# Setup of a fused cross-attention and mixture-of-experts kernel: order of the normalising, the maxima and the second batch's queries

## The chip, the cores and the metric

One core of one Trainium2 chip. The time is device microseconds of one execution, as the median of the runs shown; lower is better. TensorE is called PE in the profile, VectorE DVE, ScalarE ACT, GpSimd POOL, SyncE SP.

## The reference

```python
# x (2, 512, 128); ctx (2, 154, 128); H = 16 heads of 8; E = 8 experts, 2 chosen, capacity 160
x = x + tanh(g_xattn) * attention(layernorm(x), ctx, ctx, Wq, Wk, Wv, Wo)   # causal mask
x = x + tanh(g_ffn) * moe(layernorm(x), Wr, W1, b1, W2, b2)

# attention: softmax(where(causal, Q K^T / sqrt(8), -inf)) V, heads joined, @ Wo.T
# moe: softmax router, two experts of each token, their weights normalised, rank within an
#      expert by cumulated sum, tokens over the capacity dropped, gelu between W1 and W2
```

All in float32. The attention's queries are 512 rows for each of two batches (four tiles of 128 rows), its keys 154 (128 and 26 more). The reference's softmax subtracts the row's maximum of the scores.

## The kernel before, in words

One program with hand-written queues for each engine, ordered by semaphores. It has a setup (until 20 us), eight attention groups (20 to 72 us), and the mixture of experts (72 to 140 us). The change touches the setup and the lists of banks in the groups.

**Setup.** SP loads X for the first batch (L366), the context (L368, L369), X for the second batch (L370), WV; then, when POOL has made zeros (`zero_ready`), it clears the tables `slots` and `results` in DRAM (L374, L379). ACT issues the loads of WK and WQ (L595, L596), clears `v_all` and `top` (L599) and copies the keys (L606). DVE clears the selection matrices (L1513, L1514), does the statistics of both batches (`statistics`, L1305: four bn_stats, four bn_aggr, an add of epsilon), normalises the first (`layernorm`, L1316), splits the keys into a high and a low part (L1524, L1525), makes the masked keys of heads 0 to 5 for the maxima (L1526), normalises the second batch (L1530). The reciprocal root is a POOL power (`root`, L451). POOL makes identities and masks (L425 to L462), then after both roots the selection matrices (`packing`, L443), copies of the last context rows (L471), masked keys of heads 6 to 15 (`keys_for_max`, L474), the ones beside the values (L484 to L490), `block_mask`, the key mask `mask_k1` (L498 to L502) and `ones` (L503), which increments `consts3`; then `k1` of both batches (L507) and the masked keys of the second batch.

The PE runs matmuls on zeros (L820), the keys (L825), filling matmuls (`fill`, L805, calls L844 and L846), transposes the normalised rows (`turn_rows`, L834), makes the queries (`queries`, L826), and then alternates four packings of keys (`pack_keys`, L852; ACT copies each at L622) with seven banks of maxima (L1039 to L1053); the second batch's rows and queries and the projected values (`project_values`, L1026) lie between them. ACT copies the high half of queries (L614), DVE subtracts it for the low half (`low_queries`, L1532).

**Banks of maxima.** Two PSUM banks, `turn`, are passed between the PE and their readers in the order of the list `turns`. A bank of maxima holds the scores of one tile of 128 queries against up to four heads' masked keys (`maxima`, L865: one matmul L873, a mask on tile 0, L876, and on tile 1, L879); DVE reduces it to one maximum for each head into `top` (L1328) and frees it. Tile 0 has 128 keys and four heads (512 columns), the others 154 keys and three heads (462) or two (308). There are 22 banks for a batch, 44 in all; `shares` says how many are done in the setup (7) and beside each group (8, 6, 6, 6, 5, 5, 1), and `maxima_beside` at which of six places of the group.

**A group** is four heads of one batch. In the PE's order (L1059 to L1100): maxima at place 0, `scores` (L899), maxima at 1, `last_scores` of the last 26 keys (L910), maxima at 2, `pack` of the next group (L1018: two matmuls of the queries L886, then four of the maxima L892, for which it waits until `top` is written), maxima at 3, `values` of the group before (L920), maxima at 4, `last_values` (L933), maxima at 5. `scores` waits for ACT's copy of the pack (L644). ACT does two exponentials of a group (L681), one of the last keys (L684), then the copy of the next pack. DVE does the reductions in the same order, and between them the folds and the router.

Before group 0 the PE waits for `consts3` (L1058); the second batch's queries (L1054) and the wait for their two halves (L1070) come before `last_scores` of group 0.

Of the kernel before, what the change touches and what calls it, by code (L numbers as in the profile page):

```python
# [35 lines left out]
P = 128  # L36
B, S, D = 2, 512, 128
C = 154
# [30 lines left out]
def groups_of_heads(qt):  # L69

    if qt == 0:
        return [(4 * n, 4, P) for n in range(4)]
    return [(0, 3, C), (3, 3, C), (6, 3, C), (9, 3, C), (12, 2, C), (14, 2, C)]


def build(nc, x, ctxT, gx, gf, wqT, wkT, wvT, woT, wr, w1, b1T, w2, b2T, out):
    with ExitStack() as stack:
# [37 lines left out]
        mask_k1 = sb("mask_k1", [P, 32], BF16)  # L115
# [16 lines left out]
        kT = sb("kT", [P, B, CP])  # L132
# [110 lines left out]
        def w2_part(e):  # L243
# [12 lines left out]
        x_in = [sem(f"x_in{b}") for b in range(B)]  # L256
# [4 lines left out]
        zero_ready = sem("zero_ready")  # L261
# [55 lines left out]

        maxima_todo = [(b, qt, *h) for b in range(B) for i in range(4) for qt in range(QT)
                       for h in groups_of_heads(qt) if h[0] // 4 == i]

        shares = (7, 8, 6, 6, 6, 5, 5, 1)
        maxima_first = maxima_todo[:shares[0]]
        FIRST_HEADS = 6
# [41 lines left out]
        def _(sp):  # L365
            sp.dma_start(X[:, 0:QT, :], x_d[:, 0:QT, :]).then_inc(x_in[0], 16)  # L366
# [3 lines left out]
            sp.dma_start(X[:, QT:NT, :], x_d[:, QT:NT, :]).then_inc(x_in[1], 16)  # L370
            sp.dma_start(WV[:, :], wvT).then_inc(wv_in, 16)

            sp.wait_ge(zero_ready, 1)
# [6 lines left out]

            for g in range(TOPK):
                clear_table(g)
# [33 lines left out]
        def _(pool):  # L416
            steps = [0]

            def step(ins):
# [5 lines left out]
            pool.memset(zeros[:, :], 0.0)  # L425
            step(pool.memset(slot0[:, :], 0.0))
            step(pool.memset(slot0[:, D:D + 1], FAR))
            pool.memset(half[:, :], -0.5).then_inc(zero_ready, 1)  # L428
# [8 lines left out]
                               channel_multiplier=-1).then_inc(consts1, 1)  # L437
            step(pool.memset(minus_raw[:, :, :], 0.0))
            step(pool.affine_select(out=minus_raw[:, :, :], in_=minus_raw[:, :, :], compare_op=ALU.not_equal,
                                    fill=-1.0, base=-3 * HD, pattern=[[-32, 4], [-1, 2]],  # L440
                                    channel_multiplier=1))
# [9 lines left out]
            def root(tiles, n):  # L451
# [5 lines left out]

            step(pool.memset(mask_q[:, :, :], 0.0))
            pool.affine_select(out=mask_q[:, :, :], in_=mask_q[:, :, :], compare_op=ALU.is_ge, fill=NEG,
                               base=0, pattern=[[0, 4], [-1, P]], channel_multiplier=1)  # L460
            pool.tensor_copy(identr[:, :], identf[:, :])
            pool.tensor_copy(identb[:, :], identf[:, :]).then_inc(consts2, 1)  # L462
# [11 lines left out]
            def keys_for_max(b, h0):  # L474

                pool.tensor_tensor(kTr[:, b, h0:H],  # L476
                                   kT_part[:, 0, b, 0:C].unsqueeze(1).to_broadcast([P, H - h0, C]),
                                   head_mask[:, :, :].rearrange("p i j -> p (i j)")[:, h0:H].unsqueeze(2)
                                   .to_broadcast([P, H - h0, C]), ALU.mult).then_inc(kTr_ready, 1)

            pool.wait_ge(kT_split, 1)
            keys_for_max(0, FIRST_HEADS)

            pool.wait_ge(zeroed, 1)  # L484
            for r in range(2):
                c = ONES_AT[r]
                step(pool.memset(v0[:, :, :, :].rearrange("p b (n r) d -> p b n r d", r=2)[:, :, :, r, c:c + 1], 1.0))
                for j in range(4):
                    step(pool.memset(v1[32 * j:32 * j + C1, :, :, j, :].rearrange(
                        "p b (n r) d -> p b n r d", r=2)[:, :, :, r, c:c + 1], 1.0))  # L490
# [103 lines left out]
        def _(act):  # L594
# [41 lines left out]

            turned_rows(1)
            place_values()
            high_queries(1)

            def pack(g):

# [1119 lines left out]
```

## Time and profile before

| what | us |
|---|---|
| median of 3 runs | 143.41 |
| the runs | 142.35 to 143.93 |
| the profiled execution, its own time | 142.3 |
| its span in the profile | 140.2 |
| granted TensorE clock, mean | 0.993 of 2.4 GHz |

The span runs from the first to the last record of the profile; 2.1 us of the execution lie around it. Times of rows are microseconds from the span's start.

### The profile page before, as it was taken

Reading aid. Unit: us, or ns where it says so; the run is one execution under the profiler, and the core shown is the slowest. Engines: PE = TensorE matmul, PEld = TensorE weight load, DVE = VectorE, ACT = ScalarE, POOL = GpSimd, SP = SyncE. Lnnn points to the kernel's source line nnn. Section 1 sums busy time; section 2 is a strip of 40 time slices with the busy share of each in tenths; the row PEclk is TensorE's granted clock in tenths of the full one; section 3 lists DMA queues with packets and bytes.
Section 4 is the critical chain, followed back from the end, with each engine's and each line's share of the span. In section 5 each row is a group of like instructions: output and inputs, shape, how many; then the busy total and the mean of one; then the engine's idle time right before and its main releaser. Section 6 shows DMA issues by size and latency. Waiting matters only on the chain.

```text
span 140.2 us, 2241 instructions
## 1 busy us (share of the span) xinstructions
PE 124.4 (89%) x715; PEld 86.4 (62%) x715; DVE 103.2 (74%) x259; ACT 73.7 (53%) x134; POOL 84.0 (60%) x126
## 2 busy tenths in 40 slices
PE   5998988899899999999989989969779999989930
PEld 2443844455455646675369448959579999977620
DVE  5599845948584647377969788974399998999381
ACT  4924667166361447154827778632587678721110
POOL 6679779999999141004285788871067878773000
PEclk9999999999999999999999999999999999999997
DMA  3899880003240000000089411111740101010805
GB/s 97 257 212 222 210 269 23 0 0 99 69 134 0 5 0 0 0 0 2 0 226 314 162 58 39 39 57 55 158 114 10 45 31 43 28 35 26 293 8 150
DMA packets 19018, 12.22 MB, mean 87 GB/s; under 512 B 3381, under 2 KB 16999, under 8 KB 19008
## 3 DMA queue, kind: packets, MB, share of 16 engines
q1 hardware_dynamic: 17344, 9.59, 26.7%
q0 software_dynamic: 1088, 1.86, 4.0%
q10 hardware_dynamic: 576, 0.66, 1.3%
q8 instruction: 5, 0.08, 0.2%
q14 instruction: 5, 0.04, 0.1%
HBM read 7.25 MB, written 5.06 MB: 88 GB/s over the span
## 4 chain that ended last, share of the span: by engine, by line
PE 43%; POOL 17%; DVE 11%; DMA 11%; issue 11%; ACT 2%; SPq 2%; POOLq 1%; DVEq 0%
POOL slots L555 6%; PE turn L873 6%; PE sc L1205 5%; PE av L929 5%; DVE top L1328 4%; PE av L937 4%; PE turn L886 3%; DMA xn_all<-results 3%; PE sc L1221 3%; DMA X<-x 2%; POOL results L587 2%; PE sc L905 2%; PE turn L892 2%; POOL shared L476 2%; DMA parts_all<-slots 2%
## 5 line engine op out<-in xcount | busy, mean ns | idle before, releaser
L1328 DVE TENSOR_REDUCE top<-turn 128x3 fp32r<-128x462 f32 (+2 forms) x44 | 26.2, 606 | 13.8 <-PE turn L873 7.2
L587 POOL DMA_INDIRECT results<-p,result_of x18 | 19.8, 1099 | 12.6 <-DVE p L1630 8.1
L681 ACT ACTIVATE p_all<-sc 128x1024 f32<-128x1024 f32 x16 | 15.5, 1022 | 16.2 <-PE sc L905 16.1
L873 PE MATMUL turn<-shared,q_all 128*128 128x462 f32 (+2 forms) x44 | 20.4, 468 | 2.3 <-DVE top L1328 0.8
L555 POOL DMA_INDIRECT slots<-rows,slot_of x16 | 18.4, 1148 | 5.3 <-issue 5.0
L1205 PE MATMUL sc<-q_all,w_all 128*128 128x320 f32 x96 | 17.4, 320 | 1.2 <-issue 0.8
L752 ACT ACTIVATE late<-sc,B 128x320 f32<-128x320 f32 x32 | 15.0, 523 | 3.5 <-PE sc L1205 3.5
L1205 PEld LDWEIGHTS sc<-q_all,w_all 128*128 128x128 f32 x96 | 14.2, 188 | 2.3 <-issue 2.0
L873 PEld LDWEIGHTS turn<-shared,q_all 128*128 128x128 f32 x44 | 8.3, 189 | 11.4 <-ACT q_pack_all L644 4.7
L546 POOL TENSOR_SCALAR_AFFINE_SELECT p_all<-p_all 128x512 f32<-128x512 f32 x8 | 5.2, 646 | 16.7 <-ACT p_all L681 16.7
L1647 DVE TENSOR_TENSOR shared<-late,shared 128x640 fp32r<-128x640 f32 x16 | 13.1, 821 | 0.3
L929 PE MATMUL av<-p_all,late 128*32 128x512 f32 x64 | 8.5, 604 | 0.2 <-POOL p_all L546 0.2
L808 PE MATMUL sc<-mask_q,identb 128*128 128x512 bf16 x32 | 7.7, 380 | 0.0
L476 POOL TENSOR_TENSOR shared<-kT_part,head_mask 128x1540 fp32r<-128x1540 f32 (+1 forms) x2 | 7.1, 3534 | 0.0
L454 POOL TENSOR_TENSOR rstd<-mean_var,half 128x4 f32<-128x4 f32 x4 | 4.2, 1040 | 4.9 <-DVE mean_var L1314 3.7
L937 PE MATMUL av<-p,late 128*128 128x384 f32 x16 | 6.8, 505 | 0.0
L644 ACT ACTIVATE q_pack_all<-turn 128x512 fp32r<-128x512 f32 x8 | 4.8, 600 | 3.8 <-PE turn L892 3.8
L886 PE MATMUL turn<-q_all,pack_q 128*128 128x512 f32 x16 | 6.1, 464 | 0.4
L665 ACT ACTIVATE late<-av 128x512 f32<-128x512 f32 (+1 forms) x5 | 2.5, 511 | 6.8 <-PE av L937 6.8
L820 PE MATMUL sc<-zeros 128*128 128x512 f32 (+1 forms) x6 | 4.2, 868 | 1.5 <-POOL half L428 1.5
L538 POOL TENSOR_TENSOR w_all<-W,w_all 128x512 fp32r<-128x512 f32 x4 | 5.1, 1281 | 0.3
L892 PEld LDWEIGHTS turn<-identr,top 128*128 128x128 f32 x32 | 4.7, 190 | 1.0 <-DVE top L1328 0.3
(255 smaller groups left out, 283.1 us busy)
## 6 DMA issues: line engine op xcount, KB each, us to landing
W<-w SPq DMA_DIRECT2D x8, 256.0 KB, 3.1
p_all<-w SPq DMA_DIRECT2D x8, 256.0 KB, 5.2
slots<-slot SPq DMA_DIRECT2D x1, 1386.0 KB, 11.0
results<-zeros SPq DMA_DIRECT2D x2, 512.0 KB, 9.7
parts_all<-slots SPq DMA_DIRECT2D x5, 198.0 KB, 2.9
X<-x SPq DMA_DIRECT2D x2, 256.0 KB, 3.6
xn_all<-results SPq DMA_DIRECT2D x2, 256.0 KB, 3.9
xn_all<-results ACTq DMA_DIRECT2D x2, 256.0 KB, 4.2
```

The source lines that it names most:

```text
L476: pool.tensor_tensor(kTr[:, b, h0:H], kT_part[:, 0, b, 0:C].unsqueeze(1).to_broadcast([P, H - h0, C]), head_mask[:, :, :].rearrange("p i j ...
L555: nc.gpsimd.indirect_dma_start(out=slots, out_offset=bass.IndirectOffsetOnAxis(ap=slot_of[:, c:c + 1], axis=0), in_=rows[:, t, :], in_offs ...
L587: nc.gpsimd.indirect_dma_start(out=results, out_offset=bass.IndirectOffsetOnAxis(ap=result_of[0:m, e, n:n + 1], axis=0), in_=y[0:m, e % 2, ...
L681: act.activation(p0[:, t, heads, :], sc[:, heads, :], ACT.Exp, scale=SCALE).then_inc(sc_free, 1)
L752: act.activation(hT[:, e % 2, c, :], sc[:, c, 0:SLOTS], ACT.Gelu, bias=B1[:, e, c:c + 1]).then_inc(h_ready, 1)
L873: mm = pe.matmul(o, qT[:, 0, b, qt * P:qt * P + P], kTr[:, b, h0:h0 + nh, 0:keys], start=True, stop=(qt >= 2), skip_group_check=True)
L886: pe.matmul(ps, pack_q[:, part, i].rearrange("p j s d -> p (j s d)"), qT[:, part, b, :], start=(part == 0), stop=False, skip_group_check=True)
L929: pe.matmul(av[32 * j:32 * j + VW, :], v0[:, b].rearrange("p h d -> p (h d)")[:, at:at + VW], p0[:, g % 2, j, :], start=(g % 2 == 0), stop ...
L937: pe.matmul(av[:, P:S], v1[:, b].rearrange("p i j d -> p (i j d)")[:, at:at + 4 * VW], p1[:, g % 2, :], start=False, stop=True, skip_group ...
L1205: mm = pe.matmul(sc[:, c, 0:SLOTS], w1_part[:, e, wp, c * P:c * P + P], xsT[:, e % 2, xp, :], start=(wp == xp == 0), stop=(wp == 1))
L1328: dve.tensor_reduce(top[:, qt, h0:h0 + nh, 3 * HD], ps[:, 0:nh * keys].rearrange("p (h k) -> p h k", h=nh), AX.X, ALU.max).then_inc(turn_f ...
L1647: dve.tensor_tensor(hT_part[:, t, 1, c:c + 2, 0:SLOTS], h, hT_part[:, t, 0, c:c + 2, 0:SLOTS], ALU.subtract).then_inc(h_split, 1)
```

## The change

- X of the first batch is loaded in two pieces, tiles 0 and 1 by SP and tiles 2 and 3 by ACT's queue ahead of WK and WQ. The semaphore of the second batch is the third.
- POOL no longer makes `slot0` and the ones beside the values; DVE does (ten small memsets before the first normalising). The clearing of `slots` waits for DVE's `slot_zeros`, that of `results` for `zero_ready`.
- POOL's order: identities, head mask, `minus_raw`, the key selection matrix, `identb`, root of the first batch, `mask_q`, `identr`, the query selection matrix, the masked keys of heads 4 to 9, root of the second batch, block mask, `ident4`, a key mask of 32 partitions with one affine select, `ones`, `k1` of batch 0, masked keys of heads 10 to 15, `k1` of batch 1, masked keys of batch 1.
- DVE's order: statistics and normalising of the first batch (a signal for each tile), then the keys, masked keys of heads 0 to 3, statistics of the second batch, low queries of the first, five maxima, normalising of the second. The copy `kT` goes: ACT writes the high part of the keys itself, and DVE subtracts it from PSUM.
- PE: 3 and 3 filling matmuls for 12 and 4, with `identb` as moving operand; transposes wait for each tile; order of packings of keys and banks as below; the second batch's transposes behind the first pack (into `av`), its queries behind `last_scores` of group 0. ACT's high half of them comes after the two exponentials of group 0, DVE's low half before the reductions at place 2.
- 20 banks of maxima for a batch, 40 in all: the heads go in threes, and head 3 has one bank for tiles 1 to 3 (three matmuls of 154 columns). Five are done in the setup, and 7, 6, 6, 6, 5, 4, 1 beside the groups. With that, head 7 of tiles 1 to 3 and heads 10 and 11 of tile 3 of the first batch are reduced behind the packs that read them, which take the cleared value there.
- The mask of the last keys is placed by `ident4`, and the tanh of the gates moves behind group 0's exponentials.

```diff
-def groups_of_heads(qt):
-    if qt == 0:
-        return [(4 * n, 4, P) for n in range(4)]
-    return [(0, 3, C), (3, 3, C), (6, 3, C), (9, 3, C), (12, 2, C), (14, 2, C)]
+def units_of_maxima(b, i):
+    first = [(b, (0,), 4 * i, 4, P)]
+    if i == 0:
+        return first + [(b, (qt,), 0, 3, C) for qt in range(1, QT)] + [(b, tuple(range(1, QT)), 3, 1, C)]
+    starts = ((), (4, 7), (10,), (13,))[i]
+    return first + [(b, (qt,), h0, 3, C) for h0 in starts for qt in range(1, QT)]
...
-        shares = (7, 8, 6, 6, 6, 5, 5, 1)
+        shares = (5, 7, 6, 6, 6, 5, 4, 1)
-        FIRST_HEADS = 6
+        FIRST_HEADS = 4
+        NEXT_HEADS = 10
...
 # gpsimd
-            root((0, QT), 1)
-            root((QT, NT), 2)
-            pool.wait_ge(cleared, 1)
-            packing(pack_k, [kp for kp, qp in PRODUCTS]).then_inc(pack_ready, 1)
+            pool.wait_ge(cleared, 1)
+            packing(pack_k, [kp for kp, qp in PRODUCTS]).then_inc(pack_ready, 1)
+            pool.tensor_copy(identb[:, :], identf[:, :]).then_inc(consts2, 1)
+            root((0, QT), 1)
+            step(pool.memset(mask_q[:, :, :], 0.0))
...
-            pool.wait_ge(kT_split, 1)
-            keys_for_max(0, FIRST_HEADS)
+            pool.wait_ge(kT_ready, 1)
+            keys_for_max(0, FIRST_HEADS, NEXT_HEADS)
+            root((QT, NT), 2)
...
 # scalar
+            act.dma_start(X[:, 2:QT, :], x_d[:, 2:QT, :]).then_inc(x_in[1], 16)
             act.dma_start(WK[:, :], wkT).then_inc(wk_in, 16)
...
-            turned_rows(1)
             place_values()
-            high_queries(1)
...
             pack(0)
+            turned_rows(1)
...
                     act.activation(p0[:, t, heads, :], sc[:, heads, :], ACT.Exp,
                                    scale=SCALE).then_inc(sc_free, 1)
+                if g == 0:
+                    high_queries(1)
...
 # tensor
-            fill(sc[:, 3, :], 12)
+            fill(sc[:, 3, :], 3)
             turn_rows(0)
-            fill(sc[:, 3, :], 4)
+            fill(sc[:, 3, :], 3)
+            pe.wait_ge(wq_in, 16)
             queries(0)
...
             pack_keys(0)
-            pe.wait_ge(consts2, 1)
+            pack_keys(1)
+            pe.wait_ge(consts2, 2)
             pe.wait_ge(kTr_first, 1)
             pe.wait_ge(q_high, 1)
-            maxima(maxima_first[0:2])
-            pack_keys(1)
+            maxima(maxima_first[0:1])
+            pack_keys(2)
+            maxima(maxima_first[1:2])
+            pack_keys(3)
             maxima(maxima_first[2:3])
-            pack_keys(2)
-            maxima(maxima_first[3:4])
-            pack_keys(3)
-            maxima(maxima_first[4:5])
-            turn_rows(1)
-            maxima(maxima_first[5:6])
             project_values()
-            maxima(maxima_first[6:])
-            queries(1)
+            maxima(maxima_first[3:])
             pe.wait_ge(pack_ready, 2)
             pe.wait_ge(q_ready, 1)
             pack(0)
-            pe.wait_ge(consts3, 1)
+            pe.wait_ge(v_ready, 5)
+            turn_rows(1)
...
                 if g == 0:
                     pe.wait_ge(k_ready, 1)
-                    pe.wait_ge(q_ready, 2)
+                    pe.wait_ge(consts3, 1)
                 if g < NG:
                     last_scores(g)
+                if g == 0:
+                    queries(1)
...
 # vector
-            dve.wait_ge(x_in[0], 16)
-            statistics((0, QT), X)
-            dve.wait_ge(x_in[1], 16)
-            statistics((QT, NT), X)
-            layernorm((0, QT), X, xn, xn_ready)
+            statistics((0, QT), X, True)
...
+            ones_beside_values()
+            dve.wait_ge(rstd_ready, 1)
...
+            for t in range(QT):
+                normalised_rows(t)
...
+            statistics((QT, NT), X, True)
...
             low_queries(0)
             dve.wait_ge(zeroed, 2)
             maxima(maxima_first)
             pass_bank()
-            low_queries(1)
+            dve.wait_ge(rstd_ready, 2)
+            for t in range(QT, NT):
+                normalised_rows(t)
...
                 maxima(maxima_beside(g, 0))
                 maxima(maxima_beside(g, 1))
+                if g == 0:
+                    low_queries(1)
```

## Rows read from the trace of the kernel before

**Rows 1.** Page, busy time by engine and the group of the reductions.

```profile
PE 124.4 (89%) x715; PEld 86.4 (62%) x715; DVE 103.2 (74%) x259; ACT 73.7 (53%) x134; POOL 84.0 (60%) x126
...
L1328 DVE TENSOR_REDUCE top<-turn 128x3 fp32r<-128x462 f32 (+2 forms) x44 | 26.2, 606 | 13.8 <-PE turn L873 7.2
```

**Rows 2.** Busy time of each engine by stretch, with granted clock and DMA.

```profile
0.00:4.00 4.00, 2.48 (x3) 1.17 (x4) 1.82 (x2) 2.16 (x2) 2.56 (x17) 1.00 0.43 126
...
27.07:33.00 5.93, 5.93 (x38) 3.31 (x37) 3.58 (x9) 3.05 (x5) 5.52 (x15) 1.00 0.00 0
```

**Rows 3.** Timeline of the setup, first batch: start, length, instruction, idle before it.

```profile
4.25 0.87 DVE L1308 BATCH_NORM_STATS2 stats<-X 128x6 f32<-128x128 f32 x4 [1.19 <-DMA X<-x]
...
5.83 1.04 POOL L454 TENSOR_TENSOR rstd<-mean_var,half 128x4 f32<-128x4 f32 x1 [0.80 <-DVE mean_var L1314]
...
7.81 1.11 DVE L1321 TENSOR_SCALAR xn_all<-X,mean_var,rstd 128x128 f32<-128x128 f32 x4
...
9.68 0.60 ACT L610 ACTIVATE xn_all<-sc 128x512 f32<-128x512 f32 x1 [2.52 <-PE sc L838]
...
10.34 1.11 PE L831 MATMUL sc<-xn_all,WKQ 128*128 128x512 f32 x2
...
10.87 1.50 DVE L1321 TENSOR_SCALAR xn_all<-X,mean_var,rstd 128x128 f32<-128x128 f32 x4
...
11.49 0.60 ACT L614 ACTIVATE q_all<-sc 128x512 fp32r<-128x512 f32 x1 [1.22 <-PE sc L831]
```

**Rows 4.** Timeline from the last packing of keys to the first scores.

```profile
15.24 0.53 ACT L622 ACTIVATE w_all<-av,minus_one 128x320 fp32r<-128x320 f32 x1
...
16.03 0.60 PE L1032 MATMUL av<-WV,CT 128*128 128x128 f32 x4
...
18.46 0.56 PE L892 MATMUL turn<-identr,top 128*128 128x128 f32 x4
18.97 0.69 DVE L1534 TENSOR_TENSOR q_all<-sc,q_all 128x512 fp32r<-128x512 f32 x1 [1.00 <-ACT q_all L614]
19.11 0.60 ACT L644 ACTIVATE q_pack_all<-turn 128x512 fp32r<-128x512 f32 x1 [0.17 <-PE turn L892]
...
19.66 0.50 PE L873 MATMUL turn<-shared,q_all 128*128 128x512 f32 x1 [0.64 <-POOL ones L503]
...
20.32 0.51 PE L905 MATMUL sc<-q_pack_all,w_all 32*128 32x512 f32 x4
```

**Rows 5.** Timeline of group 0 to the second scores.

```profile
20.86 1.94 ACT L681 ACTIVATE p_all<-sc 128x1024 f32<-128x1024 f32 x2 [1.06 <-PE sc L905]
...
23.23 0.66 PE L892 MATMUL turn<-identr,top 128*128 128x128 f32 x4
...
27.07 0.50 PE L905 MATMUL sc<-q_pack_all,w_all 32*128 32x512 f32 x4
```

**Rows 6.** Chain that ended last, pieces of groups 1 to 4.

```profile
30.85 0.34 PE turn L873
...
36.54 0.41 PE turn L873
...
42.18 0.39 PE turn L892 x4
...
50.89 0.43 PE turn L873
51.32 0.23 PE turn L876
```

**Rows 7.** Groups of VectorE by form, 12 to 66 us: busy, mean ns, idle.

```profile
L1328 DVE TENSOR_REDUCE top<-turn 128x3 fp32r<-128x462 f32 x24 | 15.1, 641 | 6.1 <-PE turn L873 3.9 <-PE turn L879 2.1
L1328 DVE TENSOR_REDUCE top<-turn 128x2 fp32r<-128x308 f32 x12 | 5.7, 479 | 4.0 <-PE turn L873 3.3 <-PE turn L879 0.2
L1328 DVE TENSOR_REDUCE top<-turn 128x4 fp32r<-128x512 f32 x8 | 5.5, 692 | 3.7 <-PE turn L876 3.7
```

**Rows 8.** Groups by line, 0 to 20.3 us: busy, mean ns.

```profile
L820 PE MATMUL sc<-zeros 128*128 128x512 f32 (+1 forms) x6 | 4.2, 868 | 1.5 <-POOL half L428 1.5
...
L489 POOL MEMSET late<- 26x4 f32 x8 | 0.8, 98 | 0.5
```

More of the change, by code:

```diff
@@ L254, in build @@
         turn = [psum(f"turn{n}", [P, 512]) for n in range(2)]
-        x_in = [sem(f"x_in{b}") for b in range(B)]
+        x_in = [sem(f"x_in{n}") for n in range(3)]
         ctx_in, ctx_rep, wk_in, wv_in, wq_in, wo_in, small_in = (
@@ L423, in step @@
                 pool.wait_ge(pool_step, steps[0])
[L425 to L428, printed above, removed]
+            pool.memset(zeros[:, :], 0.0).then_inc(zero_ready, 1)
+            pool.memset(half[:, :], -0.5)
             pool.memset(identf[:, :], 0.0)
@@ L807, in fill @@
                 for _ in range(n):
-                    pe.matmul(ps, identb[:, :], mask_q[:, :, :].rearrange("p h k -> p (h k)"), start=True, stop=True,
+                    pe.matmul(ps.rearrange("p (n d) -> p n d", n=4), identb[:, :],
+                              identb[:, :].unsqueeze(1).to_broadcast([P, 4, P]), start=True, stop=True,
                               skip_group_check=True)
@@ L865, in maxima @@
             def maxima(todo):
-                for b, qt, h0, nh, keys in todo:
+                for b, tiles, h0, nh, keys in todo:
                     ps = bank()
@@ L871, in maxima @@
                         use_of["maxima", 4 * b + h0 // 4 + 1] = full[0]
[L872 to L880 removed]
+                    for n, qt in enumerate(tiles):
+                        o = ps[:, n * nh * keys:(n + 1) * nh * keys].rearrange("p (h k) -> p h k", h=nh)
+                        mm = pe.matmul(o, qT[:, 0, b, qt * P:qt * P + P], kTr[:, b, h0:h0 + nh, 0:keys],
+                                       start=(n == 0), stop=(qt >= 2), skip_group_check=True)
+                        if qt == 0:
+                            mm = pe.matmul(o, identb[:, :], mask_q[:, 0:nh, :], start=False, stop=True,
+                                           skip_group_check=True)
+                        if qt == 1:
+                            mm = pe.matmul(o[:, :, P:C], identb[:, :], mask_q[:, 0:nh, 0:C1], start=False,
+                                           stop=True, skip_group_check=True)
                     mm.then_inc(turn_full, 1)
@@ L1285, in _ @@
         def _(dve):
-            steps, uses, banks, norms = [0], [0], [0], [0]
+            steps, uses, banks, norms = [0], [0], [0], [2]
             def step(ins):
@@ L1303, in pass_bank, with statistics @@
                 banks[0] += 1
-            def statistics(tiles, src):
+            def statistics(tiles, src, landing=False):
                 for t in range(*tiles):
+                    if landing and t in (0, 2, QT):
+                        dve.wait_ge(x_in[t // 2], 16)
                     last = dve.bn_stats(stats[:, t, :], src[:, t, :])
@@ L1325, in maxima @@
             def maxima(todo):
-                for b, qt, h0, nh, keys in todo:
+                for b, tiles, h0, nh, keys in todo:
                     ps = bank()
-                    dve.tensor_reduce(top[:, qt, h0:h0 + nh, 3 * HD],
-                                      ps[:, 0:nh * keys].rearrange("p (h k) -> p h k", h=nh),
+                    n = nh * len(tiles)
+                    to = top[:, tiles[0], h0:h0 + nh, 3 * HD] if nh > 1 else top[:, tiles[0]:tiles[-1] + 1, h0, 3 * HD]
+                    dve.tensor_reduce(to, ps[:, 0:n * keys].rearrange("p (h k) -> p h k", h=n),
                                       AX.X, ALU.max).then_inc(turn_free, 1)
```

133 lines of the change are left out of this document (66 added, 67 removed).

## The prediction, made before the change was run

> **What bounds the kernel now.** I read the page first: TensorE is busy for 89% of the span, VectorE, ScalarE and GpSimd much less [rows 1]. Then the busy time by stretch: from the first scores to the last it is full. In 27.07 to 33.00 us it is busy in every microsecond, at a granted clock of 1.00, so a microsecond of matmul moved into that stretch costs nearly a microsecond [rows 2]. Third, the timeline of the first 27 us, where no engine is full and the time is a chain of handovers: X lands, statistics, root, normalise, transpose, queries, maxima, first packing, first scores [rows 3, 4]. Before the first scores, at 20.32 us, the PE also waited for POOL's constants: its first bank of group 0 started at 19.66 with `ones` named as what released it [rows 4]. Last the chain of waits: inside the groups a bank of maxima stands on it with 0.34 us where it has two heads and 0.41 to 0.43 where it has three or four [rows 6]. After group 7 nothing is edited. Everything there follows the last group, so I let it shift by whatever group 7 shifts by, and compare the landmarks "first scores" (20.32), "second scores" (27.07) and the groups 1 to 6 after them.
>
> **Setup up to the first queries.** The first root starts at 5.83 and takes 1.04, ending at 6.87, but the normalising starts only at 7.81, since VectorE did the second batch's statistics in between [rows 3]. That order is turned round. X's first tiles come in two pieces on two queues with the same bytes in all; I give that 0.1 us (between 0 and 0.3). Ten small memsets now stand on VectorE between the variance (5.6) and the root's end (6.75). No row has a small memset on VectorE; POOL's take 98 ns each [rows 8], the statistics' single steps (0.87 for four) 0.22 [rows 3]: 1.0 to 2.2 us for ten. I take 1.0, since the count of written elements is as small as POOL's; the root's 1.04 then covers it, and at the other end it would come through with 1.1 us. So normalising starts at 6.8, not 7.81: 1.0 earlier. The old one released a block of four tiles, and the copy of the turned rows started 0.76 after the last tile (8.92 to 9.68) [rows 3]; with a transpose behind each tile only the last is left, about 0.25. The copy starts at 8.2: 1.5 earlier. ScalarE issues one more DMA (the two clears and the copy of kT come 0.5 later, done by 7.7): hidden behind the normalising. Copy 0.60, queries 1.1, copy 0.60 [rows 3]: the high queries are done at 10.6 instead of 12.09.
>
> The second normalising of before ran 1.50 us for the work that took 1.11 in the first [rows 3], with POOL busy beside both; POOL's affine selects of mask_q now run beside the first. The Trainium skill (GPSIMD Engine Reference, Specifications) says why that may be: the SBUF interfaces are shared with VectorE, with contention when VectorE runs in a two-port mode or with two SBUF inputs. By the row of 1.11 the copy is at 8.2; by the rule with the row of 1.50 it is at 8.6, and the setup's gain 0.4 smaller.
>
> **From there to the first scores.** Four packings of keys end, by the last ScalarE copy (15.24 + 0.53), 3.7 after the high queries [rows 3, 4]. Now two packings stand ahead of the first bank and only one bank between the rest: copies of 0.53 one behind another with two round trips of the PE give 2.55, so 13.15. VectorE, with the second statistics (1.5 us) now ahead of the low queries, starts its maxima at 11.75; it isn't what holds this. Projected values: from 16.03 to about 17.05 [rows 4], now to 14.15. Two banks follow: 0.5 for the matmul, two reductions of 0.64 [rows 7] and a handover of 0.1, and the pack of the maxima starts at 16.05 instead of 18.46, ScalarE's copy of it at 16.65 instead of 19.11 [rows 4]. POOL has made its constants by about 14.5 (no ones beside the values, one affine select for the key mask instead of four in a chain) and k1 of the first batch by 15.6, so the wait on `ones` is gone. What is late next is the second batch: VectorE normalises it only after the fifth reduction (15.9), 1.1 us, to 17.0; its transposes stand ahead of group 0 on the PE, and from that group's first bank to the scores it is 0.66 as before (19.66 to 20.32) [rows 4]. First scores at 17.85: **2.45 us earlier**. I hold this good to 0.7 either way.
>
> **Group 0 gives most of it back.** The second batch's queries are now in the group. The PE has room for its 1.0 us. But the order of two other engines binds them: ScalarE does the high half only behind the group's two exponentials, and VectorE does the low half before the reductions of the third and fourth bank, for which the first packing of group 1 waits. From the rows: exponentials start 0.54 after the scores and last 1.94, the high queries 0.60, the low 0.69, two reductions 1.28 [rows 4, 5, 7], the pack of maxima 0.66 [rows 5], and some 0.15 of handovers: 5.85 after the first scores, at 23.7. Before it was 23.23 + 0.66 = 23.89 [rows 5], 3.6 after them. So 2.25 of the 2.45 are gone. Then one bank fewer stands before the second scores, in a stretch paced by reductions of 0.64: second scores at 26.3 instead of 27.07. **0.8 us earlier** is left.
>
> **Groups 1 to 6.** The columns of maxima are the same in all; only their place moves, together with two banks fewer in the setup, one fewer in groups 0 and 5 each. In batch 0 all reductions of two heads (479 ns) become of three (641 ns) [rows 7]; on the PE a bank of three costs 0.07 more than one of two (0.34 against 0.41), and one of four with its mask 0.43 + 0.23 = 0.66, 0.32 more than one of two [rows 6]. Going through the lists: group 1 had one bank of four and five of two, now has two of four and four of three, 0.32 + 4 x 0.07 - small masks = +0.5. Group 2 about +0.2, as its start is where VectorE is behind and two of its reductions are longer. Group 3 has the bank that holds one head for three tiles: three short matmuls instead of one. No row has this form; the nearest above is the pack's four matmuls of 128 columns in 0.39, 0.10 each [rows 6], below it is nothing beyond the columns. Three cost 0.3 against 0.2 and a small mask: +0.2 (0 to 0.3). Group 4 loses a bank of four: -0.25. Group 5: one of two fewer (-0.34), three longer (+0.2), one with a mask (+0.32), in all +0.15. Group 6: +0.05. Sum +0.85.
>
> The packs of groups 1 and 2 don't wait for all the maxima of their heads any more (head 7 of tiles 1 to 3, heads 10 and 11 of tile 3 come behind them; they are taken as cleared), so the change in order adds no wait there but the one on the bank just issued in group 1, hidden by the pack's first 0.73 us. Of POOL's later work all is earlier.
>
> **Sum.** -2.45 + 2.25 - 0.65 (the bank in group 0) + 0.85 = 0 us. The profiled execution took 142.3 us (span 140.2, 2.1 around it) and comes out at 142.3; the median of the runs was 143.41, 1.1 above it. I forecast 143.4 us, no change.
>
> **Rivals.** (A) The bank round trips are the price in the groups too. A reduction takes 0.61 us in the mean and has 0.31 of idle time before it (13.8 us over 44) [rows 1]. If that sets the groups' time and not the columns, the two banks fewer there give 0.92 each, 1.85 in place of the 0.65 of one of them, and the 0.85 of dearer columns isn't paid: with the 0.2 left of the setup that is 2.05 less, so 141.4. For it: setup and group 0 are paced so. Against it: in groups 1 to 6 the PE is full, and the banks that go take no columns with them [rows 2, 6].
> (B) Slower: the PE falls to its lower level in the setup. Twelve of the sixteen filling matmuls ahead of the first transposes and queries go, and from 6.8 us to 16 the PE has gaps. The first matmuls of before, on zeros, took 868 ns each in the mean for 512 columns or fewer [rows 8], against 1.11 for two of 512 at 10.34 [rows 3]: half the rate, though the granted clock reads 1.00 (2.4 GHz) for the first 4 us [rows 2]. At 1.2 GHz from the queries to the first pack, its matmuls on the path (queries 1.1, packings of keys, values 1.0, the pack 1.3) would take some 2 us more: 145.4. It decides if the clock is down at the first queries. The Trainium skill (TensorE: Matmul & The Clock Gate, What's actually happening) says that "the default state is throttled, and activity releases the throttle"; by that rule fewer fills can cost this, and the trace agrees in so far as the first matmuls were slow.
> (C) Slower, less: group 0's loss is as above but the normalising is late by the dear memsets (1.1) and the longer banks stall VectorE in groups 1 and 2 for another 0.5: 145.0.
> (D) The change does what it says: the second queries lie in group 0 for nothing, with the setup's whole 2.45 kept. With the bank and the dearer columns that is -2.45 - 0.65 + 0.85 = -2.25: 141.1. Against it stands only, but firmly, the order on ScalarE and VectorE.
>
> **Chances.** Forecast 0.50, A 0.17, D 0.11, B 0.09, C 0.13. A measurement of this kernel can tell about 1% (1.4 us) from no change. Faster by over 1% takes A and D: 0.28; slower takes B and C: 0.22; within: 0.50. The forecast's own range is 142.3 to 144.5; to take in 8 of 10 it goes from 141.1 to 145.2.
>
> **What would show it.** In the changed profile: normalising at 6.8 with VectorE's memsets done before; the high queries copied at 10.0; the first pack's copy at 16.65; first scores at 17.9; VectorE's low queries of the second batch started some 3.1 us after them, TensorE idle before the pack of group 1; second scores at 26.3; seventh group's scores (66.0 now) within 0.5 of that. Wrong it would be if the second scores came before 25.5 (the reductions didn't wait, or the first scores are earlier), if groups 1 to 6 took less than before (A), if the queries' two matmuls took 1.7 us or more (B), or if normalising started after 7.3 (C).

## The result and the profile after

The changed kernel takes **157.55 us** in the median (157.24 to 158.09, 4 runs), the kernel before 142.91 beside it (142.35 to 143.93). The ratio is 1.106, 95% interval 1.099 to 1.112: 10 to 11% slower. I had forecast 143.4, with 145.2 as the upper end. The runs of one kernel differ by up to 6 us with the mean granted clock of the run, so the column "undisturbed" of the table below takes the runs within 1.5% of the fastest of their kernel, and the ratios are formed over these.

The page of the changed kernel (busy time; granted clock in 40 slices; two groups by line):

```profile
span 156.1 us, 2215 instructions
...
PE 134.4 (86%) x702; PEld 91.4 (59%) x705; DVE 108.8 (70%) x266; ACT 73.7 (47%) x134; POOL 82.6 (53%) x114
...
PEclk9999965555579999999689999999999999999997
...
L1331 DVE TENSOR_REDUCE top<-turn 128x3 fp32r<-128x462 f32 (+1 forms) x40 | 25.6, 649 | 20.5 <-PE turn L874 8.3
...
L1537 DVE TENSOR_SCALAR xn_all<-X,mean_var,rstd 128x128 f32<-128x128 f32 x8 | 8.4, 1128 | 0.0
```

Two things stand out. The clock line has a hole from slice 6 to slice 12, 20 to 45 us. And the normalising, eight small instructions, takes 1128 ns each in the mean, where it took 1.11 us for the first four and 1.50 for the second [rows 3]. The chain of waits has one piece of 6.47 us in it, the longest of the chain:

```profile
14.81 1.19 DVE top L1331 x2
16.00 6.47 DVE xn_all L1537 x3
22.47 0.04 issue
22.51 0.73 PE av L837 x2
```

The timeline of the changed kernel up to the second scores (start, length, instruction, idle time of its engine before it; these answer to rows 3, 4 and 5):

```profile
6.47 1.60 DVE L1537 TENSOR_SCALAR xn_all<-X,mean_var,rstd 128x128 f32<-128x128 f32 x4
...
9.23 1.10 PE L830 MATMUL sc<-xn_all,WKQ 128*128 128x512 f32 x2
...
10.36 0.60 ACT L612 ACTIVATE q_all<-sc 128x512 fp32r<-128x512 f32 x1 [1.28 <-PE sc L830]
...
15.24 1.74 POOL L476 TENSOR_TENSOR shared<-kT_part,head_mask 128x924 fp32r<-128x924 f32 x1
...
15.91 6.80 DVE L1537 TENSOR_SCALAR xn_all<-X,mean_var,rstd 128x128 f32<-128x128 f32 x4
16.82 0.60 ACT L640 ACTIVATE q_pack_all<-turn 128x512 fp32r<-128x512 f32 x1 [1.02 <-PE turn L893]
16.93 1.04 POOL L501 TENSOR_TENSOR shared<-w_all,block_mask 128x512 fp32r<-128x512 f32 x1
...
17.20 0.30 PE L837 MATMUL av<-identf,xn_all 128*128 128x128 f32 x1 [0.48 <-DVE xn_all L1537]
...
18.07 4.31 POOL L476 TENSOR_TENSOR shared<-kT_part,head_mask 128x2464 fp32r<-128x2464 f32 x1
...
18.25 0.33 PE L837 MATMUL av<-identf,xn_all 128*128 128x128 f32 x1 [0.75 <-DVE xn_all L1537]
...
22.51 0.73 PE L837 MATMUL av<-identf,xn_all 128*128 128x128 f32 x2 [3.93 <-DVE xn_all L1537]
...
24.05 0.80 PE L906 MATMUL sc<-q_pack_all,w_all 32*128 32x512 f32 x4 [0.38 <-issue]
...
28.91 0.69 DVE L1556 TENSOR_TENSOR q_all<-av,q_all 128x512 fp32r<-128x512 f32 x1 [2.60 <-ACT q_all L612]
...
30.20 1.22 PE L887 MATMUL turn<-q_all,pack_q 128*128 128x512 f32 x2 [1.19 <-DVE top L1331]
...
35.58 0.80 PE L906 MATMUL sc<-q_pack_all,w_all 32*128 32x512 f32 x4
```

The setup of the first batch is near what I had worked out: the high queries' copy at 10.36 (10.0), the first pack's at 16.82 (16.65). Then read the POOL rows beside VectorE's four. The second and the third of the four, each asked for by itself, and the reduction ahead of them:

```profile
15.37 0.63 DVE L1331 TENSOR_REDUCE top<-turn 128x3 fp32r<-128x462 f32 x1
...
16.98 1.22 DVE L1537 TENSOR_SCALAR xn_all<-X,mean_var,rstd 128x128 f32<-128x128 f32 x1
...
17.97 4.48 DVE L1537 TENSOR_SCALAR xn_all<-X,mean_var,rstd 128x128 f32<-128x128 f32 x1
```

POOL's multiplications end at 16.98 (1.74 from 15.24), at 17.97 and at 22.38; the transposes of the first three tiles start at 17.20, 18.25 and 22.51. So each of the first three normalising instructions ended 0.1 to 0.2 us behind the POOL instruction in flight, and the third fell behind the longest, the masked keys of batch 1. The fourth, behind that one, took 0.33 us. The PE had 0.33 us of work between 18.0 and 20.0 and none in the next two. Busy time by stretch:

```profile
16.00:20.00 4.00, 1.34 (x8) 0.80 (x6) 4.00 (x3) 0.60 (x1) 4.00 (x4) 1.00 0.81 241
20.00:24.00 4.00, 1.16 (x3) 0.72 (x4) 2.71 (x2) 0.60 (x1) 3.94 (x9) 0.60 0.17 49
24.00:44.00 20.00, 18.21 (x50) 9.37 (x52) 7.79 (x13) 6.52 (x10) 9.00 (x14) 0.50 0.10 28
```

After the gap the granted clock is 0.50, 1.2 GHz, for over 20 us, though the PE is busy in 18.21 of 20: group 0 takes 11.5 us (6.75 before) and group 1 9.9 (5.1).

### The profile page after: what moved, and what is told of

Its sections match the earlier page's. It is cut to its first block, busy times and chain, and to the rows that moved or that the text cites. A ratio compares the mean times of both kernels' runs of the same rounds, so it can differ in the third digit from the quotient of the medians.

```text
span 156.1 us, 2215 instructions
## 1 busy us (share of the span) xinstructions
PE 134.4 (86%) x702; PEld 91.4 (59%) x705; DVE 108.8 (70%) x266; ACT 73.7 (47%) x134; POOL 82.6 (53%) x114
## 4 chain that ended last, share of the span: by engine, by line
PE 57%; DVE 12%; issue 8%; POOL 8%; DMA 8%; ACT 2%; SPq 1%; POOLq 1%; DVEq 0%
PE turn L874 8%; POOL slots L551 6%; PE av L930 6%; PE sc L1204 5%; PE av L938 4%; DVE xn_all L1537 4%; PE turn L887 3%; PE sc L821 3%; DMA xn_all<-results 3%; DVE top L1331 3%; PE turn L893 2%; PE sc L906 2%; PE sc L1220 2%; POOL results L583 2%; DMA parts_all<-slots 2%
## 5 line engine op out<-in xcount | busy, mean ns | idle before, releaser
L1331 DVE TENSOR_REDUCE top<-turn 128x3 fp32r<-128x462 f32 (+1 forms) x40 | 25.6, 649 | 20.5 <-PE turn L874 8.3
L874 PE MATMUL turn<-shared,q_all 128*128 128x462 f32 (+2 forms) x44 | 23.2, 554 | 1.0 <-DVE top L1331 0.6
L1204 PE MATMUL sc<-q_all,w_all 128*128 128x320 f32 x96 | 17.4, 320 | 1.5 <-issue 1.0
L874 PEld LDWEIGHTS turn<-shared,q_all 128*128 128x128 f32 x44 | 9.6, 224 | 10.9 <-issue 5.7
L930 PE MATMUL av<-p_all,late 128*32 128x512 f32 x64 | 9.4, 661 | 0.0
L887 PE MATMUL turn<-q_all,pack_q 128*128 128x512 f32 x16 | 6.7, 504 | 2.1 <-DVE top L1331 1.6
L1537 DVE TENSOR_SCALAR xn_all<-X,mean_var,rstd 128x128 f32<-128x128 f32 x8 | 8.4, 1128 | 0.0
L476 POOL TENSOR_TENSOR shared<-kT_part,head_mask 128x924 fp32r<-128x924 f32 (+1 forms) x3 | 7.8, 2590 | 0.0
L893 PEld LDWEIGHTS turn<-identr,top 128*128 128x128 f32 x32 | 5.5, 224 | 1.4 <-DVE top L1331 0.8
L837 PE MATMUL av<-identf,xn_all 128*128 128x128 f32 x4 | 1.4, 390 | 5.2 <-DVE xn_all L1537 5.2
L808 PE MATMUL sc<-identb 128*128 128x512 bf16 x22 | 5.8, 388 | 0.0
```

Of the source, the lines that this page charges most:

```text
L874: mm = pe.matmul(o, qT[:, 0, b, qt * P:qt * P + P], kTr[:, b, h0:h0 + nh, 0:keys], start=(n == 0), stop=(qt >= 2), skip_group_check=True)
L887: pe.matmul(ps, pack_q[:, part, i].rearrange("p j s d -> p (j s d)"), qT[:, part, b, :], start=(part == 0), stop=False, skip_group_check=True)
L930: pe.matmul(av[32 * j:32 * j + VW, :], v0[:, b].rearrange("p h d -> p (h d)")[:, at:at + VW], p0[:, g % 2, j, :], start=(g % 2 == 0), stop ...
L1204: mm = pe.matmul(sc[:, c, 0:SLOTS], w1_part[:, e, wp, c * P:c * P + P], xsT[:, e % 2, xp, :], start=(wp == xp == 0), stop=(wp == 1))
L1331: dve.tensor_reduce(to, ps[:, 0:n * keys].rearrange("p (h k) -> p h k", h=n), AX.X, ALU.max).then_inc(turn_free, 1)
L1537: dve.tensor_scalar(xn[:, t, :], X[:, t, :], mean_var[:, t, 0:1], rstd[:, t:t + 1], ALU.subtract, ALU.mult).then_inc(xn_ready, 1)
```

## The experiments

First and second scores, and the span, of each profiled execution; times are medians.

| kernel | first scores | second | span | time, all runs | undisturbed (of all) | ratio to before [95%] |
|---|---|---|---|---|---|---|
| before | 20.32 | 27.07 | 140.2 | 142.91 | 142.91 (4 of 4) | |
| changed | 24.05 | 35.58 | 156.1 | 157.55 | 157.55 (4 of 4) | 1.106 [1.099, 1.112] |
| e1 POOL waits | 17.83 | 26.79 | 144.5 | 145.98 | 144.4 (2 of 4) | 1.009 [0.995, 1.023] |
| e2 single heads | 18.19 | 26.87 | 146.9 | 148.15 | 143.8 (1 of 4) | none |
| e3 fills, behind the wait | 29.01 | 37.18 | 152.8 | 155.44 | 154.8 (3 of 4) | 1.084 [1.073, 1.095] |
| e4 e1 + low queries later | 17.88 | 25.03 | 140.5 | 142.61 | 142.4 (3 of 4) | 0.996 [0.987, 1.005] |
| e5 before + 40 banks | 20.27 | 26.40 | 140.9 | 144.28 | 142.9 (6 of 10) | 1.008 [1.002, 1.013] |
| e6 fills in the wait | 23.47 | 32.43 | 150.1 | 153.35 | 152.6 (3 of 4) | 1.077 [1.066, 1.088] |
| e7 e1 + queries ahead | 19.69 | 26.35 | 141.7 | 143.82 | 143.7 (7 of 10) | 1.010 [1.004, 1.016] |
| e8 low queries later | 24.13 | 33.78 | 154.0 | 154.13 | 151.9 (2 of 5) | 1.064 [1.052, 1.077] |
| e9 two inputs | 24.38 | 35.90 | 153.8 | 156.95 | 156.95 (2 of 2) | 1.104 [1.094, 1.115] |
| e10 e6 + e8 | 23.50 | 30.66 | 147.4 | 148.19 | 148.1 (4 of 5) | 1.041 [1.034, 1.047] |
| e11 e4 + std earlier | 17.84 | 24.99 | 141.6 | 142.24 | 141.9 (9 of 14) | 0.999 [0.996, 1.002] |

The second scores are 1.8 us later in e1, e6 and the changed kernel than in e4, e10 and e8, which differ from them by the place of the low queries alone.

**e1, POOL waits.** Theory L is that POOL's instructions hold VectorE's normalising, and the idle PE loses its clock.

```diff
                 if b == 0:
+                    pool.wait_ge(xn_ready, NT)
                     keys_for_max(0, NEXT_HEADS, H)
```

> The changed kernel, but POOL waits for the second batch's normalised rows behind k1 of batch 0, so none of its long multiplications runs beside them. Theory L (VectorE's normalising stands still until the POOL instruction in flight ends; the PE idles over it and falls to its lower clock): normalising takes 1.1 to 1.5 us instead of 6.8, first scores at 17.9 (24.05), second at 26.3 (35.6), granted clock 1.00 throughout, 143.4 us as in my sum. Rival O (the new order is dear in itself: second queries in group 0, longer banks): first scores earlier but groups 0 and 1 still take 10 us each and the time stays over 150.

The normalising of the second batch in e1, its PE rows in group 0, and its busy time by stretch:

```profile
15.93 1.11 DVE L1538 TENSOR_SCALAR xn_all<-X,mean_var,rstd 128x128 f32<-128x128 f32 x4
...
17.83 0.51 PE L907 MATMUL sc<-q_pack_all,w_all 32*128 32x512 f32 x4
...
20.88 0.69 DVE L1557 TENSOR_TENSOR q_all<-av,q_all 128x512 fp32r<-128x512 f32 x1 [1.41 <-ACT q_all L613]
...
22.18 0.74 PE L888 MATMUL turn<-q_all,pack_q 128*128 128x512 f32 x2 [1.55 <-DVE top L1332]
22.75 0.63 PE L894 MATMUL turn<-identr,top 128*128 128x128 f32 x4
```

The first half of L holds to the hundredth: 1.11 us, first scores at 17.83 where my sum had 17.85. Rival O falls: 11.6 us of the 14.6 are gone. But the clock was not 1.00. In e1's profile the granted clock is 0.94 in 20 to 24 us and 0.50 in 24 to 28; its four runs lie between 143.5 us (mean clock 0.99) and 146.8 (0.96). The gap of 1.55 us ahead of `pack` is group 0's wait for the second queries. Two of the four runs have a mean clock of 0.96, so the part of L that gave the clock to the rows' stall alone was too narrow. That this wait brings the clock down is supported by e4 below, which takes it away, and not settled: e3 has the same gap at a clock of 1.00.

**e2, single heads.** POOL's two long multiplications as 22 short ones, one head each.

```diff
                 if b == 0:
-                    keys_for_max(0, NEXT_HEADS, H)
+                    for h in range(NEXT_HEADS, H):
+                        keys_for_max(0, h, h + 1, h == H - 1)
...
-            keys_for_max(1, 0, H)
+            for h in range(H):
+                keys_for_max(1, h, h + 1, h == H - 1)
```

The last argument, new in the helper, lets only the last piece of a batch signal.

> The changed kernel, with POOL's masked keys of heads 10 to 15 and of batch 1 made one head at a time (22 instructions of about 0.27 us in place of two of 1.74 and 4.31). Theory L: a normalising instruction is held at most for one POOL instruction, 1.04 (k1) at worst and else 0.3, so the four end by about 18.2 and the PE's gap is short; clock 1.00, 143.5 to 145 us. Rival S (POOL and VectorE share a bandwidth, so that the four are slow in proportion to POOL's work): normalising still ends at 21 or later and the time stays over 152.

The four in e2, and the first of POOL's pieces beside them:

```profile
15.20 2.51 POOL L476 TENSOR_TENSOR shared<-kT_part,head_mask 128x154 fp32r<-128x154 f32 x6
...
15.87 1.52 DVE L1541 TENSOR_SCALAR xn_all<-X,mean_var,rstd 128x128 f32<-128x128 f32 x4
```

POOL does the same multiplications beside VectorE, in pieces of 0.45 us (0.27 expected), and the four end at 17.4 instead of 22.7, none longer than 0.48. The hold lasts for an instruction, not for an amount of work: rival S falls. One run, at a mean clock of 0.99, took 143.79 us, as expected; the other three, at 0.945 to 0.961, took 147.3 to 149.0, with the same fall of the clock as in e1 (granted 0.50 in 28 to 34 us in the profile).

**e3 and e6, filling matmuls while the PE waits.** In e3 I put 18 of them ahead of the fourth transpose; the long wait is ahead of the third, so they ran behind it and only delayed. e6 puts them right.

```diff
                 for t in range(QT):
+                    if b:
+                        fill(sc[:, 3, :], (2, 4, 18, 0)[t])
                     pe.wait_ge(xn_ready, QT * b + t + 1)
```

> The changed kernel, with 28 filling matmuls more on the PE while it waits for the second batch's rows (2, 4, 4 and 18 ahead of its four transposes). The stall stays: first scores at 24 to 24.5. Theory L, its second half (the lower clock is the larger part): clock 1.00 in 20 to 44 us, group 0 takes 8.5 and group 1 5.7 instead of 11.5 and 9.9, and the time is 143.4 + 6.2 = about 149.6. If the stall alone were the price, nothing would change: 157.

> The changed kernel with 24 filling matmuls on the PE while it waits for the second batch's rows, 18 of them ahead of the third transpose, where the long wait is (in e3_fills they stood ahead of the fourth, behind the wait, and only delayed it). The stall stays: first scores at 24.1. Theory L: clock 1.00 past 20 us, then 48.4 us of groups as in e4 plus 2 for group 0's own wait, total 149.5 to 151. If the lower clock were not the larger part: 155 or more.

The pack of group 1 in e3 and in e6:

```profile
33.35 0.73 PE L889 MATMUL turn<-q_all,pack_q 128*128 128x512 f32 x2 [1.54 <-DVE top L1333]
...
27.81 0.73 PE L889 MATMUL turn<-q_all,pack_q 128*128 128x512 f32 x2 [1.54 <-DVE top L1333]
```

e3 tells two things in spite of its misplaced fills. From its first scores to the end it takes 152.8 - 29.0 = 123.8 us, the changed kernel 156.1 - 24.05 = 132.05, and e3's granted clock is 1.00 from 28 us on. Of these 8.2 us, 6.9 lie in groups 0 and 1 (8.17 and 6.31 us in e3, 11.53 and 9.87 in the changed kernel): that is the low clock behind the stall. Another 1.6 lie in group 6, where the changed kernel's clock falls once more (last section). e3's own clock was down to 0.62 in 24 to 28 us and back behind the 18 matmuls, where the changed kernel's came back only at 44 us. And e3 has group 0's wait of 1.54 us without a fall of the clock.

In e6 the first scores come at 23.47, at full clock up to 28 us; then it is 0.60 in 28 to 34 and 0.54 in 34 to 40. This comes behind group 0's wait, here at 26.3 to 27.8 us and as long as in e3, and the time is 2 to 4 us above what I expected. So the same wait was followed by the low clock in one profile and not in the other; what else it takes wasn't tried.

**e4, low queries later.** Built on e1.

```diff
                 maxima(maxima_beside(g, 1))
-                if g == 0:
-                    low_queries(1)
...
                 for n in (3, 4, 5):
                     maxima(maxima_beside(g, n))
+                if g == 0:
+                    low_queries(1)
```

> As e1_pool_waits, and VectorE takes the low half of the second batch's queries behind the last maxima of group 0 instead of ahead of the third and fourth bank. My step on group 0 (ScalarE's and VectorE's order there gives back 2.25 us): against e1 second scores come about 2 us earlier, 24.3 instead of 26.3, and the time is 141.4 to 142. If that step was wrong, nothing changes against e1.

The same pack of group 1 in e4, and the second scores:

```profile
21.21 0.74 PE L888 MATMUL turn<-q_all,pack_q 128*128 128x512 f32 x2 [0.53 <-DVE top L1332]
...
25.03 0.51 PE L907 MATMUL sc<-q_pack_all,w_all 32*128 32x512 f32 x4
```

The pack starts 1.0 earlier and the second scores come 1.8 earlier than in e1, against 2 expected. The granted clock is 1.00 from the start to 120 us. The time, 142.61, can't be told from the kernel before (ratio 0.996, interval 0.987 to 1.005): all of the loss of 14.6 us is gone with one wait added on POOL and one instruction of VectorE moved. The gain of 141.4 to 142 that I expected is not shown.

**e5, the lists of banks alone**, put into the kernel before.

```diff
-        shares = (7, 8, 6, 6, 6, 5, 5, 1)
+        shares = (5, 7, 6, 6, 6, 5, 4, 1)
...
-        maxima_todo = [(b, qt, *h) for b in range(B) for i in range(4) for qt in range(QT)
-                       for h in groups_of_heads(qt) if h[0] // 4 == i]
+        maxima_todo = [u for b in range(B) for i in range(4) for u in units_of_maxima(b, i)]
```

> The kernel before with the 40 banks and their shares alone (five in the setup), its order otherwise untouched. By the terms of my sum: one or two banks' 0.3 to 0.6 us less in the setup, the bank of group 0 -0.65, groups 1 to 6 +0.85: within 0.7 us of before. Rival A (each bank that goes is worth its round trip of 0.92): 2 to 3.7 us faster. If the dearer banks cost what groups 1 to 6 show in e4 (45.7 us between first and last scores before, 48.4 there): 1 to 2 us slower.

0.8% slower, interval 0.2 to 1.3%. Group by group against before: group 0 -0.62, then +1.04, +0.48, -0.05, -0.21, +0.27, 0.00. The setup gave nothing, as its end waits for POOL's constants [rows 4]. Rival A falls. The chain of waits of e5 shows where groups 1 and 2 lose:

```profile
27.41 0.65 DVE top L1332
28.06 0.04 issue
28.10 0.73 PE turn L888 x2
...
32.78 0.53 DVE std L1581
33.31 0.15 DVE centre L1582
33.46 0.02 issue
33.49 0.65 DVE top L1332
```

Where the chain of before went from the bank straight into the pack at 28.5, a reduction of three heads now stands ahead of it; and at group 2's start the longer reductions meet the router's two instructions.

**e7, queries ahead of group 0.** Built on e1, with the second batch's queries behind its transposes on all engines.

```diff
             turn_rows(1)
+            queries(1)
...
-                if g == 0:
-                    queries(1)
```

> As e1_pool_waits, but the second batch's queries stand ahead of group 0 on all engines, as they did before the change, so that group 0 has no wait for them. First scores about 0.3 to 1.9 later than 17.83 (transposes, copy, queries 1.1 on the PE ahead of the first bank): 19 to 19.7. If the queries inside group 0 were the price of e1 (146.0): group 0 takes 6.7 us or less, the clock stays at 1.00, and the time is 142 to 143.5. If not, it is as e1 or later.

First scores at 19.69, group 0 in 6.66 us, granted clock 1.00 through to 120 us, 143.82 us, 0.3 above what I expected. That fits group 0's wait as the price of e1, but weakly: only one of these ten runs has a mean clock as low as 0.96, against two of e1's four, and over the undisturbed runs the two kernels are 0.8 us apart. Standing ahead costs what it saves: the second scores come at 26.35, 1.3 later than in e4.

**e8, low queries later, nothing else; e10, that with e6's fills.**

> The changed kernel with VectorE's low half of the second queries behind group 0's last maxima, and nothing else (POOL does not wait). It tells how the two waits share the loss: the long one at 18 to 22.4 us is still there. Theory L: normalising ends at 22.7, first scores at 24.1, the clock still falls at 20 us, group 0 loses its own wait of 2 to 3 us (more at the lower clock): 153 to 155. If group 0's wait were what brings the clock down: 148 or less.

> The changed kernel with the 24 filling matmuls of e6 and the later low queries of e8 together: the stall of the rows stays, both idle times of the PE are gone. It prices the stall alone. Theory L: first scores at 23.5, clock 1.00 throughout, second scores 7.15 later as in e4 (30.6), total = e4's 142.6 + 5.6 = 148.2. If the lower clock comes all the same: over 151.

e8's five runs spread from 151.5 to 155.9 us (mean clocks 0.956 to 0.916). The median of all, 154.13, is inside the expectation, the undisturbed two, 151.9, are 1.1 below it; none is near the 148 of the other reading. e10 was to price the stall of the rows alone, and does: expected 148.2, measured 148.19 in the median. Its busy time by stretch, for the stall and behind it:

```profile
16.00:20.00 4.00, 4.00 (x22) 2.00 (x21) 4.00 (x3) 0.60 (x1) 4.00 (x4) 1.00 0.94 257
20.00:24.00 4.00, 3.95 (x21) 1.65 (x19) 3.10 (x3) 0.60 (x1) 3.93 (x9) 1.00 0.12 36
```

The stall is as long as in the changed kernel, but the PE is busy over it with matmuls that nobody reads, and the clock stays at 1.00 through group 1. e8, without these matmuls, has 0.50 in 20 to 28 us. The two profiled executions are 6.6 us apart in span, 6.0 of it in groups 0 and 1 (9.65 and 9.85 us in e8, 7.16 and 6.30 in e10).

**e9, two inputs in place of the pointer form.**

```diff
-                dve.tensor_scalar(xn[:, t, :], X[:, t, :], mean_var[:, t, 0:1], rstd[:, t:t + 1],
-                                  ALU.subtract, ALU.mult).then_inc(xn_ready, 1)
+                dve.scalar_tensor_tensor(xn[:, t, :], X[:, t, :], mean_var[:, t, 0:1],
+                                         rstd[:, t:t + 1].to_broadcast([P, D]),
+                                         ALU.subtract, ALU.mult).then_inc(xn_ready, 1)
```

> The changed kernel with the normalising as scalar_tensor_tensor (the root as a second input from SBUF, broadcast) in place of tensor_scalar with two pointers. It tells which form of VectorE's instruction is held by POOL's. If only the two-port mode of a single-input instruction is held (H1): the four take some 0.9 to 1.2 us in all beside POOL, first scores at 18, time 143 to 147. If an instruction with two SBUF inputs is held as well, as the Trainium skill has it (GPSIMD Engine Reference, Specifications: contention with both) (H2): again 6 to 7 us for the four and 155 to 158.

The same four in e9, and the POOL instruction beside the third:

```profile
15.89 7.15 DVE L1537 SCALAR_TENSOR_TENSOR xn_all<-X,mean_var,rstd 128x128 f32<-128x128 f32 x4
...
18.30 4.30 POOL L476 TENSOR_TENSOR shared<-kT_part,head_mask 128x2464 fp32r<-128x2464 f32 x1
```

H2: an instruction with two inputs from SBUF is held just as well. The Trainium skill (GPSIMD Engine Reference, Specifications) names instructions with two SBUF inputs, beside those in a two-port mode, as the ones that contend with GpSimd; the trace agrees, with 7.15 us for four. Whether the pointer form ran in a two-port mode no run here shows. Not held, in the changed kernel's trace beside POOL's multiplication of 9.75 to 11.47: the aggregates at 9.97 (four in 0.38). Held there: the 4-element add of epsilon behind them, 1.11 us for 0.17.

**e11, std earlier.** Built on e4: the router's two instructions stand in VectorE's idle time of group 1.

```diff
                 for n in (3, 4, 5):
                     maxima(maxima_beside(g, n))
+                    if g == 1 and n == 3:
+                        dve.wait_ge(rstd_ready, 2)
+                        dve.tensor_tensor(std[:, :], mean_var[:, :, 1], rstd[:, :], ALU.mult)
...
```

> e4_low_later, and VectorE's two instructions for the router (std, centre) stand in its idle time of group 1 behind place 3, not ahead of group 2's first reductions. In e4 they lie on the chain with about 0.7 us at the start of group 2. If that is what group 2 lost (7.27 against 6.78 before), group 2 is 0.5 to 0.8 shorter and the time 0.5 to 0.8 below e4, 141.9. If they are held by POOL's weight splitting there, nothing comes of it: 142.6.

Group 2 is 6.75 long instead of 7.27 as hoped. The time is 142.24 over 14 runs, ratio 0.999 [0.996, 1.002]: level with the kernel before. No kernel of the study is faster than it beyond its interval.

## Why the prediction was wrong

**The step that failed** is this: "What is late next is the second batch: VectorE normalises it only after the fifth reduction (15.9), 1.1 us, to 17.0". It began at 15.91 and took 6.80. I had the rule in hand and priced it by the wrong row: the 1.50 of rows 3 was the normalising beside POOL's short selects, so I allowed the first batch a possible 0.4, which the sum left out, and the second nothing. I never asked which instruction POOL would be in at 16 us. By my own sum it had finished `k1` of batch 0 at 15.6, so the masked keys of heads 10 to 15 (1.74 us) were in flight at 15.9, with `k1` of batch 1 (1.04) and the masked keys of batch 1 (2464 elements, 4.31) behind them. Each hold carried the next normalising instruction into the next of the three. "Of POOL's later work all is earlier" stands there as a comfort; it was the cause. e1, e2 and e9 show it: without a long POOL instruction in flight the four take 1.11 us, beside pieces of 0.45 us 1.52, and with two inputs from SBUF 7.15.

**The second half was in rival B, at another place.** B had the clock fall in the setup for want of fills. It didn't: the granted clock is 1.00 up to 20 us with 6 fills instead of 16. It fell when the PE stood idle for 3.93 us, and the rows of before have no idle time of this length behind 10 us, so the price could only come from B's reading that the low level doubles a matmul: the second queries' two took 2.08 us at 0.50 in the changed kernel and 1.12 at full clock in e1. (B's other reading, that the matmuls on zeros ran at half the rate, is too strong: six of them took 4.2 us together, 0.70 each, against 0.55 for one of the queries, at the same granted clock of 1.00, so they show no lower level.) The ladder of e4, e10, e8 and the changed kernel prices it, by undisturbed runs: the stall alone takes 142.4 to 148.1, +5.7; the clock behind it takes that to 151.9, another +3.8 (5.9 by the medians of all runs, 6.6 between the two profiles); and group 0's own wait, with what it does to the clock, takes it to 157.55, +5.7 (3.4 by the medians of all runs), where e6 against e10 has 4.5. How much of the last two terms is the gap and how much the clock differs from run to run, and whether they add is not shown.

**The setup** came near what I had worked out: normalising from 6.47 (6.8), but 1.60 us long beside POOL's selects for my 1.11; keys' last copy ended 13.29 (13.15); first scores without the hold 17.83 (17.85). The earlier start and the longer normalising nearly cancel, so the agreement to the hundredth is partly luck. The statistics started 0.8 earlier, at 3.47, not 0.1, and the root ended at 6.09. But the ten memsets, 0.83 in all (1.0 expected), wait for ScalarE's clear and run from 5.60 to 6.43. They were not hidden: they set the start of the normalising, and ate 0.35 of that 0.8.

**Group 0** gave back what I said: pack of group 1 ended at 23.38 in e1 (23.7), and taking that step away (e4) moved the second scores by 1.8 (2.0 expected). But it was worth more than its 2 us in the runs in which the low clock followed it. Rival D, the second queries for nothing, needs e4's order; even there the second scores' lead of 2.0 us over before is spent by group 6.

**Groups 1 to 6** were priced too low: +1.53 in e5 for my +0.85. The sum of PE terms was near in groups 3 to 6; what it lacked is that groups 1 and 2 have two places where a reduction of 0.64 stands on the chain. (By the lists one reduction of group 2 is longer, not two, as I had it.) From second to eighth scores e4 takes 2.3 us more than before; 1.5 of it is e5's, the other 0.8 isn't settled.

**Rival C** named dear memsets and longer banks. The first were cheap; the second are the 0.7 us above, a small part of the loss.

## What to carry to other kernels

Before you move work of VectorE, write down which GpSimd instruction will be in flight at its new time, and how long it is: a short instruction from SBUF can wait for all of it, as the normalising did here (0.33 us became 4.48). Split long GpSimd instructions (e2), or hold them back by a semaphore (e1), where VectorE is on the chain. And price an idle gap of the PE on the path not by its length alone: here a stall of 5.7 us cost 3.8 to 6.6 more at the lower clock. Matmuls that nobody reads, put into the gap, saved that part (e10 against e8). A gap of 1.54 us was followed by the low clock in e1, e2 and e6 and not in e3.

## What the runs showed of the hardware that I had not expected

The hold goes by instruction: a normalising of 0.33 us took 4.48 beside one POOL multiplication of 4.31, 1.22 beside one of 1.04. Reductions from PSUM went on unhindered: the one at 15.37 took 0.63 us with POOL's 1.74 in flight, as in rows 7 (0.64).

The granted clock also falls where the PE is busy without a gap. In the changed kernel's profile (from the end of group 5 through most of group 6):

```profile
74.00:76.00 2.00, 2.00 (x12) 1.05 (x12) 1.72 (x16) 0.86 (x1) 0.00 (x0) 0.86 0.00 0
76.00:78.00 2.00, 2.00 (x9) 1.36 (x7) 0.56 (x1) 1.46 (x3) 0.63 (x1) 0.50 0.00 0
78.00:80.00 2.00, 2.00 (x15) 1.80 (x18) 0.91 (x2) 0.08 (x1) 0.00 (x0) 0.79 0.00 0
```

Ahead of it the PE ran 16 matmuls of 8 columns between 72.4 and 74.3 us (the router's). Group 6 took 7.2 us there against 5.4 before. The profiled runs of e2, e8, e10 and e11 show the same, with a group 6 of 7.1 to 7.2 us; e1, e3 to e7, e9 and before don't (5.4 to 5.6), with the same matmuls. It may be what spreads the runs: of before's 17 runs beside e11, those with a mean clock of 0.989 or more took 141.5 to 142.7 us, the others (0.974 to 0.984) 143.8 to 145.8. What decides between the two wasn't tried.
